# Rotary tables made in the tile loop of the first mixture, x loaded first, and the opening's norm and gate work shared out anew

## The reference

```python
x = jnp.concatenate([q, k, v], axis=-1)
ig = (x @ Wi + bi)            # input gate, 16 heads
fg = (x @ Wf + bf)            # forget gate
log_f = jax.nn.log_sigmoid(fg)
# cumulative sums of log_f, a causal matrix of log D, its row maximum
C = qk * jnp.exp(log_D - max_log_D)
normalizer = jnp.maximum(jnp.abs(C.sum(-1)), jnp.exp(-max_log_D))
h = (C / (normalizer + EPS)) @ v   # then a norm per head
```

```python
inv_freq = 1.0 / THETA ** (jnp.arange(0, HD, 2) / HD)
freqs = pos[:, None, :, None] * inv_freq
return x * jnp.cos(emb) + _rotate_half(x) * jnp.sin(emb)
```

## Time and profile before

| | us |
|---|---|
| three runs | 1381.02, 1383.56, 1390.79 |
| median | 1383.56 |
| profiled execution, its own time | 1384.76 |
| its span | 1382.9 |
| mean granted clock of TensorE in it | 0.888 of full |

### The profile page before, as it was taken

One profiled execution on the slowest core, in us unless ns is written; L12 is line 12 of the kernel. 1 busy time (PEld: TensorE's weight loads), 2 busy tenths in 40 slices (PEclk: granted clock), 3 DMA queues, 4 the chain that ended last, 5 costly groups with the idle time before them and its releaser, 6 DMA issues.

```text
span 1382.9 us, 22666 instructions
## 1 busy us (share of the span) xinstructions
PE 1154.0 (83%) x8105; PEld 850.6 (62%) x8128; DVE 866.9 (63%) x1958; ACT 586.2 (42%) x1327; POOL 350.9 (25%) x315
## 2 busy tenths in 40 slices
PE   1684677799985599888999998999468999999985
PEld 0463355444443366488998864677356888888753
DVE  6677797677785464335565568544486766666565
ACT  3433153366673232234434343222244755555352
POOL 1313000222211200213122214777502322224132
PEclk8655698899995799999999988999788999999998
DMA  7200001700003220500000035533530000000000
GB/s 234 86 2 2 0 1 30 329 2 1 2 2 110 84 84 36 200 8 1 1 1 1 1 123 236 180 113 100 179 128 1 1 1 1 1 1 1 15 32 31
DMA packets 40762, 81.68 MB, mean 59 GB/s; under 512 B 6672, under 2 KB 30096, under 8 KB 38736
## 3 DMA queue, kind: packets, MB, share of 16 engines
q1 hardware_dynamic: 35376, 65.84, 13.1%
q0 software_dynamic: 5280, 14.42, 3.2%
HBM read 65.31 MB, written 16.91 MB: 59 GB/s over the span
## 4 chain that ended last, share of the span: by engine, by line
PE 63%; DVE 15%; issue 4%; ACT 4%; DMA 2%; POOL 1%; DVEq 0%; SPq 0%; ACTq 0%; POOLq 0%
PE psum L1903 4%; PE psum L2757 4%; PE psum L2795 4%; PE psum L2309 4%; PE psum L1875 4%; PE psum L2767 4%; PE psum L2329 3%; PE psum L1499 3%; PE psum L2739 2%; PE psum L2719 2%; PE psum L1157 2%; PE psum L1828 2%; PE psum L3096 2%; PE psum L1517 2%; PE psum L1806 2%
## 5 line engine op out<-in xcount | busy, mean ns | idle before, releaser
L1318 DVE TENSOR_REDUCE c_max<-psum 128x2 f32<-128x512 f32 x128 | 81.5, 678 | 21.6 <-PE psum L1132 20.2
L1218 ACT ACTIVATE c_probs<-psum 128x512 f32<-128x512 f32 x128 | 75.1, 602 | 43.1 <-PE psum L1143 43.1
L2795 PE MATMUL psum<-a_wo,a_outT 128*128 128x256 f32 x256 | 75.1, 405 | 0.7 <-DVE x_tok L2979 0.7
L1903 PE MATMUL psum<-a_wo,a_outT 128*128 128x256 f32 x256 | 75.2, 407 | 0.0
L2309 PE MATMUL psum<-m_experts,m_tileT 128*128 x188 | 63.6, 461 | 1.7 <-DVE m_tileT L2537 1.7
L2862 ACT ACTIVATE a_probs<-psum,a_max,a_q_rstd 128x128 f32<-128x128 f32 x128 | 56.9, 457 | 17.3 <-DVE a_max L2924 17.2
L1957 ACT ACTIVATE a_probs<-a_probs,a_max 128x64 f32<-128x64 f32 x128 | 42.7, 334 | 44.9 <-DVE a_max L2013 44.9
L1875 PE MATMUL psum<-ctxT_yT_hi,a_wq 128*128 128x128 f32 x256 | 52.5, 288 | 8.2 <-DVE a_qT L1999 7.1
L258 PE MATMUL psum<-ctx_tok,ident_f 128*128 128x512 f32 x58 | 32.0, 706 | 31.1 <-DMA m_rows<-y_tok,m_slot 18.2
L1999 DVE TENSOR_TENSOR a_qT<-psum,a_columns 128x512 f32<-128x512 f32 x32 | 22.0, 687 | 54.9 <-PE psum L1875 54.9
L1499 PE MATMUL psum<-m_w,m_tileT 128*128 x120 | 54.3, 595 | 2.3 <-DVE m_tileT L1659 2.3
(11 more groups left out here) (548 smaller groups left out, 3383.3 us busy)
## 6 DMA issues: line engine op xcount, KB each, us to landing
m_w<-m_w SPq DMA_DIRECT2D x8, 1536.0 KB, 16.6
m_experts<-m_e SPq DMA_DIRECT2D x16, 608.0 KB, 12.1
a_wq<-a_wq SPq DMA_DIRECT2D x2, 2048.0 KB, 12.1
a_wo<-a_wo SPq DMA_DIRECT2D x2, 2048.0 KB, 11.8
m_rows_back<-m_back SPq DMA_DIRECT2D x4, 1024.0 KB, 9.0
a_trig<-trig_sin_cos SPq DMA_DIRECT2D x1, 2048.0 KB, 6.3
ctxT_yT_hi<-f_gate_up SPq DMA_DIRECT2D x2, 1024.0 KB, 7.4
a_sin_cos<-a_trig SPq DMA_DIRECT2D x1, 2048.0 KB, 9.6
```

Of the source, the lines that this page charges most:

```text
L1218: e.activation(c1P[:, n % 8, :, :], ps[:, 2 + n % 2, :].rearrange("p (k t) -> p k t", k=2), ACT.Exp, scale=float(1.0 / np.sqrt(np.float32( ...
L1318: e.tensor_reduce(c1M[:, u % 2, j, :], ps[:, c1_score_bank(n), :].rearrange("p (q t) -> p q t", q=2), AX.X, ALU.max).then_inc(c1_mx, 1)
L1903: ins = e.matmul(ps[:, 7, 0:D], a2at[:, i % 2, h, :, :], a2wo[:, h, :], start=(h == 0 and g is None), stop=(h == HQ - 1), skip_group_check ...
L2795: ins = e.matmul(ps[:, 7, 0:D], a3at[:, i % 2, h, :, :], a3wo[:, h, :], start=(h == 0 and g is None), stop=(h == HQ - 1), skip_group_check ...
```

## The change

The rotary tables leave the setup. Their four loads are issued by SP in the first mixture behind the row tiles. VectorE computes the angles in four pieces of 512 columns behind tiles 9 to 12 (keys in two pieces, then queries), ScalarE the sines of 1024 columns behind tiles 11 and 13, SP stores them before the stores of tiles 10 and 12. The buffers are `ctxT_yT_hi` (reduced angles, then cosines) and `ctxT_yT_lo` (turns, then sines); the positions lie in `y_tok`.

```diff
+        TRIG_LOADED = 16 * 4
+        TRIG_DVE_AT = {9: (0, 0), 10: (0, 1), 11: (1, 0), 12: (1, 1)}
+        TRIG_ACT_AT = {11: 0, 13: 1}
+        TRIG_OUT_AT = {10: 0, 12: 1}
...
+            e.dma_start(trig_kp[:, :], a["a3_kpos"]).then_inc(trig_in, 16)
+            e.dma_start(trig_row[:, :], a["a3_rows"][0:1, 0:S].broadcast_to([P, S])).then_inc(trig_in, 16)
+            e.dma_start(trig_col[:, :], a["a3_freq"]).then_inc(trig_in, 16)
+            e.dma_start(trig_pos, a["itok"].unsqueeze(0).broadcast_to([P, N])).then_inc(trig_in, 16)
             for t in range(TILES):
+                if t in TRIG_OUT_AT:
+                    x = TRIG_OUT_AT[t]
+                    e.wait_ge(*trig_sc.at(2 * x + 2))
+                    e.wait_ge(trig_in, TRIG_LOADED + 32 * x)
+                    e.dma_start(a["a3_trig"][:, x, 0, :], trig_trn[:, x, :]).then_inc(trig_in, 16)
+                    e.dma_start(a["a3_trig"][:, x, 1, :], trig_red[:, x, :]).then_inc(trig_in, 16)
...
+            def sines(x):
+                e.wait_ge(trig_f, x + 1)
+                e.activation(trig_trn[:, x, :], trig_red[:, x, :], ACT.Sin).then_inc(trig_sc.sem, 1)
+                act_step(e, e.activation(trig_red[:, x, :], trig_red[:, x, :], ACT.Abs))
+                e.activation(trig_red[:, x, :], trig_red[:, x, :], ACT.Sin, bias=trig_q[:, 0:1], scale=-1.0).then_inc(trig_sc.sem, 1)
...
+            def angles(x, h):
+                own = slice(h * HALF, (h + 1) * HALF)
+                red, trn = trig_red[:, x, own], trig_trn[:, x, own]
+                if (x, h) == (0, 0):
+                    e.wait_ge(trig_in, TRIG_LOADED)
+                    e.memset(trig_q[:, :], float(np.pi / 2))
+                    dve_step(e, e.tensor_copy(trig_kpf[:, :], trig_kp[:, :]))
+                if x == 0:
+                    batches = slice(h * B // 2, (h + 1) * B // 2)
+                    dve_step(e, e.tensor_tensor(red.rearrange("p (b t) -> p b t", t=S), bc(trig_kpf[:, batches], 2, S), bc(trig_row[:, :], 1, B // 2), ALU.mult))
+                else:
+                    dve_step(e, e.tensor_copy(red, trig_pos[:, own]))
+                    dve_step(e, e.tensor_scalar(red, red, trig_col[:, 0:1], None, ALU.mult))
+                dve_step(e, e.tensor_scalar(trn, red, 1.0 / (2 * np.pi), None, ALU.mult))
+                dve_step(e, e.tensor_scalar(trn, trn, ROUND, -ROUND, ALU.add, ALU.add))
+                dve_step(e, e.scalar_tensor_tensor(red, trn, -TWO_PI_HI, red, ALU.mult, ALU.add))
+                dve_step(e, e.scalar_tensor_tensor(red, trn, -TWO_PI_LO, red, ALU.mult, ALU.add))
+                dve_step(e, e.tensor_scalar(red, red, PI, -PI, ALU.min, ALU.max))
```

```diff
         def setup_sync(e):
+            for h in range(2):
+                e.dma_start(xt[:, 4 * h:4 * h + 4, :], a["x"][4 * h * P:(4 * h + 4) * P, :].rearrange("(t p) d -> p t d", p=P)).then_inc(x_in[h], 16)
             e.dma_start(identf[:, :], a["ident"]).then_inc(loaded, 16)
...
         def setup_act(e):
             e.wait_ge(loaded, LOADED)
+            act_step(e, e.activation(gates[:, :], gates[:, :], ACT.Tanh))
             turn_act(e, 0, cTh)
...
-            finish(e, 1)
+            e.sem_inc(stage_done, 1)
...
+            for i in range(NT):
+                if i % 4 == 0:
+                    e.wait_ge(x_in[i // 4], 16)
+                ins = e.bn_stats(st6[:, i, :], xt[:, i, :])
+            dve_step(e, ins)
+            ln_shift(e, 0, NT, l0_ln)
```

```diff
+            for bank, cols in ((0, slice(32, 64)), (1, slice(0, 32))):
+                gate_part(bank, cols, KC, 6, cTh, cTl)
+                if bank == 0:
+                    wait_yT(e, 1)
+                gate_part(bank, cols, 0, KC, yTh, yTl).then_inc(l0_g, 1)
...
         def l0_act(e):
-            turn_act(e, 1, yTh)
+            e.activation(va[:, :, :, 0:DH0], ct[:, :, :].rearrange("p t (h d) -> p t h d", h=NH0), ACT.Copy).then_inc(l0_va, 1)
+            e.wait_ge(*l0_ln.at(1))
+            ln_normalised(e, 0, NT)
+            turn_act(e, 1, yTh, 4)
...
+            e.wait_ge(yTh_ready, 8)
+            q_by_head(0)
+            q_by_head(1)
+            act_step(e, e.activation(T_[:, 0:1], l0bi[:, 1:2], ACT.Exp))
+            e.wait_ge(l0_g, 1)
+            act_step(e, e.activation(T_[:, :], ps[:, 0, 0:L0_T], ACT.Abs, bias=l0bi[:, 1:2]))
+            e.sem_inc(l0_f, 1)
             act_step(e, e.activation(T_[:, :], T_[:, :], ACT.Exp, scale=-1.0))
             e.activation(T_[:, :], T_[:, :], ACT.Ln, bias=1.0).then_inc(l0_l, 1)
+            q_by_head(2)
+            q_by_head(3)
...
-            ln_dve(e)
-            turn_dve(e, 1, yTh, yTl)
+            turn_dve(e, 0, cTh, cTl)
+            turn_dve(e, 1, yTh, yTl, 4)
+            for n in range(4):
+                cc, h2 = n // 2, n % 2
+                e.tensor_scalar(Ql[:, cc, h2, :], yTl[:, cc, :], l0hm[:, h2:h2 + 1], None, ALU.mult).then_inc(l0_ql, 1)
+            e.wait_ge(l0_f, 1)
+            dve_step(e, e.tensor_scalar(E_[:, :], ps[:, 0, 0:L0_T], l0bi[:, 1:2], 0.0, ALU.add, ALU.min))
```

220 lines of the change are left out of this document (85 added, 135 removed).

## The result

The changed kernel takes **1367.8 us** (median of 4 runs, 1366.1 to 1371.5) against 1385.3 (4 runs, 1381.0 to 1390.8) of the kernel before beside it: 17.5 us less, ratio 0.988, 95% interval 0.9845 to 0.9912. The forecast was 1361.6, 22.0 less, the range 1355 to 1371. The profiled execution took 1367.2 us (span 1365.4), 17.5 less span than before.

What follows compares the result with a forecast made beforehand. The opening is bound by a chain of loads, VectorE and ScalarE steps, the tile loop by TensorE. Opening gain 22.6 us less 0.6 lost in the tile loop: 22.0 off 1383.6 gives 1361.6 us, range 1355 to 1371.

Steps and rivals of the forecast that it cites:

- checkpoint: End of VectorE's scans (max log d) in the opening: 53.81 us before, forecast 31.2 us, a gain of 22.6 us.
- Loads: Opening: with x first and the table loads gone, ctx lands at 10.0 us, bounds 8.5 and 13.7.
- Rival 1: Loads hold the opening, x first gives nothing: gain 18.9 us or a little less, 1365 to 1368 us; chance 0.13.
- Norms on ScalarE: Opening: eight normalising activations of 256 columns replace VectorE's eight, 0.33 us each, 2.7 us in all, ending at 19.0.
- Exp's table load: Opening, ScalarE ahead of the softplus: table load and a one-column Exp take 1.5 us, to 24.8.
- Scans: End of the opening: VectorE's work after Ln takes 3.76 us as today, from 27.4 to 31.2.
- Head loop: Half-clock loop after the opening: no gain, with 3 us put into the range for other clock edges.
- ScalarE in the tile loop: First mixture: sines plus two table loads take 5.7 us against 4.57 idle; overhang 1.1 us twice, 0.6 us lost.
- Rival 2: Each table switch in the tile loop costs more than its load: 3 us lost, 1364 to 1367 us; chance 0.05.
- Queues: Tile loop: the added table loads and stores on SP cost 0, at most 3 us if the second store pair held the queue.
- Rivals 3 and 4: Clock falls in tile loop: 1389 us, chance 0.04; tables moved but not hidden: 1387 us, chance 0.02 (half exposed 0.06).
- Theory C: From the follow-ups: the change's own table work, DMAs and stores in the loop cost the 4.7 us lost behind the opening.

Runs made afterwards that it cites:

- pool_back: Changed kernel with the value copy and q's low parts given back to GpSimd; 1362.5 us, one run, end of the opening's scans at 30.05 us.
- c1_fillers: Changed kernel with more TensorE filler products at the second attention's entry; 1389.18 us, ratio 0.9843 to the kernel before, on the slower chip.
- best2: Changed kernel with norms on VectorE before its ctx wait, ctx's low parts before the casts, and added fillers at the second attention's entry; 1353.99 us, ratio 0.9773.
- x_behind_ctx: Changed kernel with the two loads of x put behind the load of ctx; 1366.6 us, one run, end of the opening's scans at 30.59 us.
- barrier_back: Changed kernel with the barrier behind the setup put back, ctx's low parts ahead of it; 1362.8 us, one run, opening's scans end at 31.90 us.
- norm_on_vector: Changed kernel with the eight norms on VectorE and ScalarE's value copy behind the gates; 1358.79 us, ratio 0.9794 to the kernel before.
- tables_only: Kernel before with only the rotary tables, their loads and stores moved to the tile loop; 1407.82 us, ratio 0.9982, on the slower chip.
- loads_late: Changed kernel with the mixtures' router loads and the zeroing of m_rows back ahead of the first layer's loads; 1371.7 us, one run.
- after_again: The changed kernel once more, no edit, on the slower chip; 1393.89 us, ratio 0.989 to the kernel before.

## Why the prediction was right

The mechanism and the place were right: the opening's chain got shorter, the tile loop took the tables for nothing. The checkpoint came within 0.4 us of its forecast, the total 4.5 us short of its own (17.5 of 22.0). Several steps were off and cancelled, so that the checkpoint is that close is in part luck.

- *Loads.* ctx landed at 10.9, not 10.0 (issued at 3.27 as thought, but 7.6 us on the way; bounds 8.5 to 13.7). Rival 1 did not happen, though in part it was near: VectorE waited 3.10 us for the last of the gates' loads, a wait that I had not in the sum; it was hidden behind ScalarE.
- *Tanh.* I let its table load run behind ctx's landing, 1.28 us. It runs at 0.73, since it waits for nothing. That gave nothing: in my sum too the transposes came last there.
- *Norms on ScalarE.* **The mis-sized term: 4.03 us, not 2.7.** I priced a 256-column pass at 0.33 in a row, from copies without operand pointers. The first of them alone takes 0.59, each further one 0.50. The Trainium skill, ScalarE: Activation LUTs, section What ACT_TABLE_LOAD costs, adds about 93 ns for each of the two per-partition operands, which gives 0.59 for this pass; the row agrees.
- *Gates.* First bank read at 25.48. About 24 was forecast; the norms made it late.
- *Exp's table load* is not there: the one-column Exp at 25.15 takes 0.19. The Trainium skill, ScalarE: Activation LUTs, section Table sets: the hidden batching unit, lists tanh with exp in one set, and the rows agree with that. It still took 1.28 us at 26.50 to come from Exp to Ln.
- *Scans.* Abs to Ln's end 2.7 us as priced; then 0.5 us to hand over to VectorE, and 2.9 us from 28.74 to the end. Together 3.4 instead of 3.76, since the first scan took 0.69 and not 1.49. GpSimd's passes beside it are the likely reason for the 1.49, but pool_back's scans were short beside them.
- *Checkpoint* 31.59 against 31.2: +0.8 (ctx) +1.3 (norms) -1.4 (Exp's table load, not there) +0.1 (ScalarE waits for the gates) -0.4 (scans), and the small ones.
- *Head loop* 0: right, the offset is 22.2 through it. *VectorE in the tile loop* 0: right, a half took 3.5 us (516.27 to 519.80) and the tile copy came 0.16 behind it.
- *ScalarE in the tile loop*, 0.6 us lost: **wrong, 0.0**. The two table loads of each half (2.6 us) are not there. Rival 2, each switch costing more than its load, fell with them; the drain that the Trainium skill, ScalarE: Activation LUTs, section What ACT_TABLE_LOAD costs, adds to a load had nothing to show itself on. On the opening's load the rows hold no drain: the load at 26.50 ends at 27.78, Ln starts at 27.80.
- *Queues* 0: right. Rivals 3 and 4 did not happen: clock 1.00 in the loop, period 6.05.
- *The sum.* **Its mis-sized term is the one that the forecast put at nothing**: 22.2 at the checkpoint against 22.6, and then 17.5 in the end. The 4.7 us between lie outside the steps, in the range's term for other clock edges. I had put 3 us on it and thought of the head loop; it was the second attention's entry (3.6 us) and the second mixture's (2.8), of which 2.3 came back further on. By the number alone rival 1 (1365 to 1368) fits better than the forecast; only the rows, ctx at 10.9 and the checkpoint at 31.6, say that it was not that.

**What stays open.** That the second attention's entry is slow by the clock is shown (c1_fillers, best2). Why it falls in one execution and not in another is not: of the twelve traces without added fillers nine have 20.4 us or more there, one 18.3, and only before and x_behind_ctx 16.5 to 16.8, at checkpoints of 53.8 and 30.6. The second mixture's entry changes form independently of it, and no run took that one apart. The kernel before has a single trace, and its total scatters too (1379.8 to 1391.0 us on the faster chips), so how much of the 4.7 us belongs to these two executions is not known; the medians are 17.5 us apart as well. On the faster chips the stretch from checkpoint to end lies between 1315 and 1330 us in kernels that differ only in their opening (and best2's fillers), more than the two entries explain. The early gate products of ctx were read off (3.84 against 1.2 us of wait), not undone by themselves. The hand-over from Ln to VectorE took 0.5 us in the changed kernel and 0.1 in barrier_back and norm_on_vector; no run says why. Theory C's stores and loads in the loop were in every one of these kernels; barrier_back and norm_on_vector, which have them too, lose nothing.

## What to carry to other kernels

A change with five parts is not five gains: read which row each part's wait ends at. Here two of them (statistics ahead of the late loads, foreign loads behind the stage's own) made most of the new order's gain; of two others, x first gave nothing that shows and the value copy on ScalarE cost 1.4 us. Put what is on the longest chain on the engine that idles there: the norms in VectorE's 3 us wait took 2.8 and 4.1 us more off the opening than the same norms behind ScalarE's copies. Repeat the trace of one kernel before you read a difference of 1 us off two of them: one load that lands late moves the whole chain, here by up to 2.7 us. And when an early stage gets shorter, look at the granted clock at the entry of every stage behind it before you believe the difference; the added filler products at one entry gave 4.8 us there, more than the opening's last refinements.

## What the runs showed of the hardware

- A Sin behind a Silu needs no table load (519.36 Silu, 520.74 Sin, and no load between), nor does an Exp behind a Tanh. Loads of 1.28 us stand between Exp and Ln.
- A VectorE cast from fp32 to bf16 that meets a GpSimd memset or copy ends 0.1 to 0.2 us behind it: 2.01 us for 128 columns that take 0.23 (pool_back), 2.01 for 384 that take 0.36. The Trainium skill, SBUF — State Buffer, section Who interferes with whom, calls this an exclusive hold of a shared port pair for a whole instruction; the casts agree. The scans fit less well: of two alike beside GpSimd's passes in tables_only one took 0.69, the other 1.60. In each of the three traces with these passes one VectorE step is held, and it ends 1.6 to 1.8 us behind the start of a pass: the first scan at 52.10 (pass from 50.31, before), the second at 44.56 (42.91, tables_only), l_max_log_d at 30.06 (28.33, pool_back).
- An issue on SP's queue is mostly 0.4 to 0.7 us, but the eighth load took 2.8 us to issue in the changed kernel (4.48), and in loads_late the issue right behind the zeroing of 2 MB took 5.5. All loads behind it start later by that.
- The same ctx load, with the same loads ahead of it, landed between 10.0 and 12.2 us (c1_fillers, after_again).
- One chip of three took 22 to 26 us longer for the kernel before and the changed one, nearly all of it in the second mixture: from 850 to 950 us TensorE is busy 86 us there and 99 on the other chip, at the same clock (0.96 and 0.97).
- The clock of 1.00 in the first 22 us of the changed kernel is no measurement: its trace has no record of the clock ahead of 23.8 us. The gate products start 0.21 us apart in fours up to 23.7 and 0.11 apart from 23.9 on, which is half and then full rate.
